# Head-by-head value products, earlier branch numbers and directly loaded gather indices in a two-layer graph network kernel

## The chip, the core and the metric

One core of one Trainium2 chip runs the whole program in one launch. The metric is the device time of one execution in microseconds.

## What is computed

Two graph layers over 6250 nodes of 160 channels (64 scalars and 32 vectors of three) and 200000 edges sorted by destination. What matters of the reference (LN and the matrices between are left out):

```python
# layer 0: attention
msg = (s_n @ Ws_src)[src] + (s_n @ Ws_dst)[dst]
w1 = rbf @ W_rbf
m1_s, m1_v = _cg_tp(msg_s, msg_v, y0, y1, w1[...])
a = jnp.sum(leaky((m1_s @ W_alpha).reshape(e, H, AS_)) * alpha_dot, axis=-1)
ex = jnp.exp(a - segment_max(a, dst)[dst]); alpha = ex / segment_sum(ex, dst)[dst]
m2_s, m2_v = _cg_tp(val_s, val_v, y0, y1, w2...)
h = concatenate([m2_s @ Ws_vlin, m2_v @ Wv_vlin])      # 4 heads of 40 columns
agg = segment_sum(alpha * h, dst)
# layer 1: mean over the edges of each destination
w = silu(edge_scalars @ Wfc1) @ Wfc2
e0, e1 = f0[src], f1[src]
n0..n3 = segment_mean(w * e * sh, dst)
```

## The kernel before, in words

**Groups.** Edges are taken in groups of 512 (four tiles of 128, edge on partition). Layer 0 has 391 groups, layer 1 has 392, two to a pair. Since the edges are sorted by destination, the sums of a group fall into a window of 128 nodes' worth of blocks, and a group whose nodes span more takes extra windows, in a loop behind a branch (`more_of` L663, `more_count` L660).

**Layer 0** runs under `schedule(step)` (L486): each of the five engines has its own program of the same steps, a step handles group g in several depths, and semaphores alone tie the engines together. In a step:

- SP (loads, one queue): `load_dst` L679 (destinations spread to all partitions, dst_bc), `load_y` L682, and `load_edge` for group g+4 (L674 to L676: rbf on 8 blocks of partitions, y twice), which waits until POOL has made the product edge of group g+2.
- POOL (gathers): `add_message` (L730, msg = got_src + got_dst of group g+2), `take_idx` (L714, copies the indices of group g+4 from the resident table idx_all into a small buffer and waits for its own copy), four indirect gathers (L720: two tiles, from src_tab and dst_tab), `scale_edge` (L737, edge = rbf * y), four more gathers. Eight gathers and two tensor operations to a group.
- PE: edge weights (`weigh` L767), transposes of msg (L773), `add_piece` L778, logits and weights turned (L791, L796), `sum_products` L802 (all 4 value parts times the softmax weights, summed into the window, 128 rows of which 32 belong to each head), and `project` L809, which multiplies the copied sums (held) by the value matrices. Its output has the four heads side by side, and of these the product of a head's rows with the other heads' columns is not used.
- DVE: `take_window` L990 picks from it, in four operations of 32 partitions, each head's own columns times two masks (side); `add_sums` L998 adds them to the running sums. It also makes blocks (L1030), product (L1053 and around), gated (L1134), near (L1095) and far (L1069, from dst_bc).
- ACT: copies out of PSUM, exponentials.

**Layer 1** runs under `by_fours(step)`. SP loads rbf, y_edge and 2 KB of indices to a group (L1463); POOL gathers four tiles (L1497); PE makes weights (L1516, L1527) and window sums (L1538); DVE makes to_node L1616, pre (L1625, L1629), along and val (L1641, L1647). After each second group DVE merges a pair's window into total (`merge`, `add_window` L1653, two operations): it reads the block number from a table in SBUF into a register (L1658), adds, then reads two window numbers (`more_of_pair` L1339, L1340) and branches; PE reads the same two and branches.

Of the kernel before, what the change touches and what calls it, by code (L numbers as in the profile page):

```python
# [15 lines left out]
I32 = mybir.dt.int32  # L16
ALU = mybir.AluOpType
# [494 lines left out]
def layer0(nc, ctx, A, K):  # L512
# [4 lines left out]
        "edge0", "edge1", "edge_y0", "edge_y1", "dst0", "dst1", "got0", "got1", "indexed", "summed", "scaled",  # L517
# [6 lines left out]
    with ExitStack() as sx:  # L524
# [120 lines left out]
        win = psum[3][:, 512:512 + HEADS * SB].rearrange("p (h c) -> p h c", h=HEADS)  # L645
# [22 lines left out]
        with nc.Block() as block:  # L668
            @block.sync
            def _(sp):  # L670
# [12 lines left out]

                def step(g, slot, use, now, mid, late):
                    if not now:
                        return
                    if not mid:
                        for first in range(2):
                            load_edge(first, first)
                        load_y(0, 0)  # L690
                        for first in range(2):
                            wait_apart(sp, s["scaled"], first + 1, s["tick_s"])
                            load_edge(first + 2, first)
                    if late:
                        wait_apart(sp, s["top"], g, s["tick_s"])
# [12 lines left out]
            def _(pool):  # L708
# [30 lines left out]
                def step(g, slot, use, now, mid, late):  # L739
# [12 lines left out]
                for first in range(2):  # L752
                    take_idx(first, first)
                    gather(first, range(TILES))
                for first in range(2):
                    add_message(first, first, 0, True)
                    scale_edge(first, first, 0, True)
                    take_idx(first + 2, first)
# [5 lines left out]
            def _(pe):  # L764
# [41 lines left out]
                def project():  # L806
                    for b in range(4):
                        cols = slice(0, SB) if b == 0 else slice(AS, HV)
                        last = nc.tensor.matmul(win[:, :, cols], held[:, P * b:P * b + P], w_val[:, b, :, cols],  # L809
                                                start=b == 0, stop=b == 3)  # L810
                    return last

                def step(g, slot, use, now, mid, late):
# [20 lines left out]
                    if late:  # L834
                        pe.wait_ge(s["sum_copied"], g - 1)
# [14 lines left out]
                        more_of(pe, g - 2, more_count(pe, g - 2), more)  # L850
# [116 lines left out]
            def _(dve):  # L967
# [869 lines left out]
```

## Time and profile before

| | us |
|---|---|
| median of 3 runs | 8944.23 (8936.49 to 8950.29) |
| the profiled execution | 8938.21 |
| its span | 8936.4 |
| PE busy in the span | 7983.1 (89%) |
| DVE busy | 7351.8 (82%) |
| POOL busy | 5977.1 (67%) |
| ACT busy | 3272.5 (37%) |

The span is one profiled execution; the rows below are of it. PE is matmul, PEld its weight loads (they overlap with PE), POOL the gathers and two tensor operations, SP the loads. A busy share is a mean over stages with different limits. Layer 0 runs from about 364 to 6255 us, layer 1 from about 6590 to 8870 us.

### The profile page before, as it was taken

Reading aid. Unit: us, or ns where it says so; the run is one execution under the profiler, and the core shown is the slowest. Engines: PE = TensorE matmul, PEld = TensorE weight load, DVE = VectorE, ACT = ScalarE, POOL = GpSimd, SP = SyncE. Lnnn points to the kernel's source line nnn. Section 1 sums busy time; section 2 is a strip of 40 time slices with the busy share of each in tenths; the row PEclk is TensorE's granted clock in tenths of the full one; section 3 lists DMA queues with packets and bytes.
Section 4 is the critical chain, followed back from the end, with each engine's and each line's share of the span. In section 5 each row is a group of like instructions: output and inputs, shape, how many; then the busy total and the mean of one; then the engine's idle time right before and its main releaser. Section 6 shows DMA issues by size and latency. Waiting matters only on the chain. (4 is left out here: it accounts for less than half of the span.)

```text
span 8936.4 us, 202775 instructions
## 1 busy us (share of the span) xinstructions
PE 7983.1 (89%) x50701; PEld 6094.9 (68%) x50702; DVE 7351.8 (82%) x18803; ACT 3272.5 (37%) x8375; POOL 5977.1 (67%) x5890
## 2 busy tenths in 40 slices
PE   2699999999999999999999999787968888888888
PEld 1488888888888888888888888666634444444445
DVE  4699999999999999999999999675368888887886
ACT  1244444444444444444444444332222222222223
POOL 0577777777777777777777777551046666666664
PEclk9799999999999999999999999898568888888888
DMA  3344444444444444444444433220012222222222
GB/s 54 78 99 99 98 98 99 98 99 98 99 98 99 98 98 99 99 98 99 98 99 98 99 98 98 66 70 23 11 43 65 64 65 65 64 65 64 65 64 58
DMA packets 616620, 725.49 MB, mean 81 GB/s; under 512 B 284132, under 2 KB 390884, under 8 KB 616573
## 3 DMA queue, kind: packets, MB, share of 16 engines
q0 software_dynamic: 225408, 385.00, 19.6%
q1 hardware_dynamic: 391165, 339.92, 15.0%
q8 instruction: 22, 0.36, 0.0%
q14 instruction: 25, 0.20, 0.0%
HBM read 708.40 MB, written 16.06 MB: 81 GB/s over the span
## 5 line engine op out<-in xcount | busy, mean ns | idle before, releaser
L720 POOL DMA_INDIRECT got_src<-src_tab,idx x1564 | 1773.3, 1134 | 659.3 <-POOL idx L714 358.4
L778 PE MATMUL bank_pair<-w_msg,blocks 128*128 128x160 f32 (+2 forms) x15640 | 2067.2, 288 | 61.3 <-DVE blocks L1030 61.3
L778 PEld LDWEIGHTS bank_pair<-w_msg,blocks 128*128 128x128 f32 x15640 | 1975.2, 192 | 100.3 <-DVE blocks L1030 95.5
L1497 POOL DMA_INDIRECT gotf<-f_tab,idx x1568 | 1536.2, 980 | 758.0 <-issue 466.2
L720 POOL DMA_INDIRECT got_dst<-dst_tab,idx x1564 | 1499.0, 958 | 529.3 <-issue 505.5
L802 PEld LDWEIGHTS bank_pair<-weights_t,product 128*128 128x128 f32 x12896 | 1496.5, 195 | 309.3 <-issue 294.9
L802 PE MATMUL bank_pair<-weights_t,product 128*128 128x128 f32 x12896 | 1573.3, 281 | 8.9 <-ACT weights_t L929 8.2
L1538 PE MATMUL bank_pair<-val,to_node 128*128 128x385 f32 x3136 | 1328.5, 573 | 2.7 <-DVE val L1647 2.7
L1589 ACT ACTIVATE val<-pre,y_edge 128x160 f32<-128x160 f32 x1568 | 542.7, 417 | 1618.6 <-DVE pre L1629 1614.7
L1538 PEld LDWEIGHTS bank_pair<-val,to_node 128*128 128x128 f32 x3136 | 658.1, 221 | 593.1 <-issue 348.7
L767 PE MATMUL bank_pair<-edge,w_edge 64*128 64x512 f32 x3128 | 884.8, 642 | 5.0 <-DVE blocks L1030 5.0
L936 ACT ACTIVATE rl<-bank_pair 128x256 f32<-128x256 f32 x391 | 150.2, 384 | 1801.9 <-PE bank_pair L778 1801.9
L1527 PE MATMUL bank_pair<-w_fc,hid 64*128 64x192 f32 x3136 | 399.1, 376 | 315.7 <-DVE val L1647 306.4
L897 ACT ACTIVATE product<-gated,y_edge 128x96 f32<-128x96 f32 x1564 | 458.1, 363 | 573.4 <-DVE gated L1134 573.2
L1527 PEld LDWEIGHTS bank_pair<-w_fc,hid 64*128 64x128 f32 x3136 | 272.7, 202 | 565.8 <-DVE val L1647 424.3
L737 POOL TENSOR_TENSOR edge<-rbf,y 128x512 f32<-128x512 f32 x391 | 500.8, 1281 | 234.6 <-PE bank_pair L778 227.5
L809 PEld LDWEIGHTS bank_pair<-w_val,held 128*128 128x128 f32 x3224 | 412.2, 190 | 307.2 <-ACT held L902 307.2
L730 POOL TENSOR_TENSOR msg<-got_src,got_dst 128x640 f32<-128x640 f32 x391 | 607.4, 1554 | 16.0 <-PE bank_pair L767 8.9
L990 DVE TENSOR_TENSOR win_scaled<-bank_pair,side 32x82 f32<-32x82 f32 x1612 | 384.8, 239 | 188.2 <-PE bank_pair L809 129.6
L1030 DVE TENSOR_TENSOR blocks<-bank_pair,turned_low 128x512 f32<-128x512 f32 x782 | 500.8, 680 | 32.5 <-PE bank_pair L767 28.1
L1030 DVE TENSOR_TENSOR blocks<-bank_pair,turned_high 128x512 f32<-128x512 f32 x782 | 502.1, 683 | 24.7 <-PE bank_pair L767 19.7
L1616 DVE TENSOR_TENSOR to_node<-iota_row,slot 128x512 f32<-128x512 f32 x392 | 270.6, 690 | 274.1 <-PE bank_pair L1538 141.7
(265 smaller groups left out, 12830.9 us busy)
## 6 DMA issues: line engine op xcount, KB each, us to landing
rbf<-in_rbf SPq DMA_DIRECT2D x391, 256.0 KB
dst_bc<-in_dst_rows SPq DMA_DIRECT2D x391, 256.0 KB
y<-in_y SPq DMA_DIRECT2D x391, 128.0 KB
y<-in_y SPq DMA_DIRECT2D x391, 96.0 KB
gotf<-f_tab,idx POOLq DMA_INDIRECT x1568
got_src<-src_tab,idx POOLq DMA_INDIRECT x1564
got_dst<-dst_tab,idx POOLq DMA_INDIRECT x1564
rbf<-in_rbf SPq DMA_DIRECT2D x392, 32.0 KB
```

The costliest lines, as they stand in the source:

```text
L720: pool.indirect_dma_start(out=buf[slot][:, t, :], out_offset=None, in_=table[:, :], in_offset=bass.IndirectOffsetOnAxis(ap=idx[slot][:, c: ...
L730: pool.tensor_tensor(msg[slot][:], got_src[slot][:], got_dst[slot][:], ALU.add).then_inc(s["summed"], 1)
L737: pool.tensor_tensor(edge[slot][:], rbf8[slot][:], y8[slot][:], ALU.mult).then_inc(s["scaled"], 1)
L767: nc.tensor.matmul(ebank[half], w_edge[r, pair, :], weigh.operand[r, :], start=True, stop=True).then_inc(s["weighed"], 1)
L778: return nc.tensor.matmul(to, blocks[rows, k, P * t:P * t + P], w_msg[rows, c0:c1], start=start, stop=stop)
L802: last = nc.tensor.matmul(sum_bank[:, P * b:P * b + P], product[slot][:, t, b, :], weights_t[:, t, :], start=t == 0, stop=t == TILES - 1)
L897: last = nc.scalar.activation(product[slot][:, t, 1:4, 64:96], gated[:, t, CS:D].rearrange("p (x c) -> p x c", x=3), ACT.Copy, scale=y_edg ...
L1030: dve.tensor_tensor(blocks[:, k, :], ebank[k % 2], (turned_low, turned_high)[k // 2][:], ALU.mult).then_inc(s["block_done"], 1)
L1497: pool.indirect_dma_start(out=got[k][:, t, :], out_offset=None, in_=f_tab[:, :], in_offset=bass.IndirectOffsetOnAxis(ap=idx[k][:, t:t + 1] ...
L1527: last = nc.tensor.matmul(weights[k % 2][:, t, 0:192], hid[k % 2][r, P * (t % 2):P * (t % 2) + P], K["w_fc2"][r, :], start=True, stop=True)
L1538: last = nc.tensor.matmul(win[k // 2], to_node[k % 2][:, t, :], val[k][:, t, :], start=k % 2 == 0 and t == 0, stop=k % 2 == 1 and t == TIL ...
L1589: last = nc.scalar.activation(val[k][:, t, 0:D], pre[:, t, 0:D], ACT.Copy, scale=y_edge[k][:, t, 0:1])
```

## The change

Three parts.

**Value products by head.** `project` (now L818) makes, for each of its 4 parts, four matmuls: head h's 32 columns of held as weights, that head's 41 or 24 value columns as the moving side, out to PSUM rows 32h to 32h+31. `take_window` is one operation on 128 partitions.

**Gather indices of layer 0.** POOL's copy and its wait go. SP loads 128 x 8 indices (4 KB) from DRAM into the same two small buffers, four groups ahead, at the head of its step; POOL waits for that load, then for msg (summed).

**Branch numbers.** In layer 0 PE reads its count ahead of the wait for sum_copied. In layer 1 block number and count are packed in one table (marks1); each engine reads one number early, and the second only inside the branch.

```diff
-        win = psum[3][:, 512:512 + HEADS * SB].rearrange("p (h c) -> p h c", h=HEADS)
+        win = psum[3][:, 512:512 + SB]
...
+                def load_idx(g, slot):
+                    sp.dma_start(idx[slot][:], group_of(A["idx"], g)).then_inc(s[f"idx{slot}"], 16)
+
                 def step(g, slot, use, now, mid, late):
...
                         for first in range(2):
+                            load_idx(first, first)
+                        for first in range(2):
                             load_edge(first, first)
                         load_y(0, 0)
                         for first in range(2):
+                            wait_apart(sp, s[f"got{first}"], 128, s["tick_s"])
+                            load_idx(first + 2, first)
+                        for first in range(2):
                             wait_apart(sp, s["scaled"], first + 1, s["tick_s"])
                             load_edge(first + 2, first)
+                    if not (isinstance(g, int) and g + 4 >= NG):
+                        wait_apart(sp, s[f"got{slot}"], use * 128 + 256, s["tick_s"])
+                        load_idx(g + 4, slot)
                     if late:
                         wait_apart(sp, s["top"], g, s["tick_s"])
                     load_dst(g, slot)
...
-                def take_idx(g, slot):
-                    pool.tensor_copy(idx[slot][:], idx_all[:, bass.ds(g, 1), :].rearrange("p a c -> p (a c)")).then_inc(s["indexed"], 1)
-                    wait(s["indexed"], g + 1)
...
                     add_message(g + 2, slot, use + 1, False)
                     if further:
-                        take_idx(g + 4, slot)
+                        wait(s[f"idx{slot}"], use * 16 + 48)
                         wait(s["summed"], g + 3)
                         gather(slot, (0, 1))
...
-                        last = nc.tensor.matmul(win[:, :, cols], held[:, P * b:P * b + P], w_val[:, b, :, cols],
-                                                start=b == 0, stop=b == 3)
+                        for h in range(HEADS):
+                            r = slice(BLK * h, BLK * h + BLK)
+                            last = nc.tensor.matmul(win[r, cols], held[:, P * b + BLK * h:P * b + BLK * h + BLK], w_val[:, b, h, cols],
+                                                    start=b == 0, stop=b == 3)
...
                     if late:
+                        count = more_count(pe, g - 2)
                         pe.wait_ge(s["sum_copied"], g - 1)
                         project().then_inc(s["projected"], 1)
...
-                        more_of(pe, g - 2, more_count(pe, g - 2), more)
+                        more_of(pe, g - 2, count, more)
...
-                    for h in range(HEADS):
-                        r = slice(BLK * h, BLK * h + BLK)
-                        last = dve.tensor_tensor(win_scaled[r, :, :], win[r, h, :].unsqueeze(1).broadcast_to([BLK, 2, SB]),
...
-                    return last
+                    return dve.tensor_tensor(win_scaled[:], win.unsqueeze(1).broadcast_to([P, 2, SB]),
+                                             side[:, at_group(g), :].rearrange("p a c -> p (a c)").unsqueeze(2).broadcast_to([P, 2, SB]),
+                                             ALU.mult)
...
-def more_of_pair(eng, more_from, q):
-
-    return (eng.value_load(more_from[0:1, at_pair(q)], min_val=0, max_val=MAX_W),
-            eng.value_load(more_from[0:1, at_pair(q + 1)], min_val=0, max_val=MAX_W))
+def more_of_pair(eng, more_from, q, count, body):
+
+    with eng.If(count > 0):
+        first = eng.value_load(more_from[0:1, at_pair(q)], min_val=0, max_val=MAX_W)
+        body(first, first + count)
...
+        def mark_of(eng, q):
+            return eng.value_load(marks[0:1, at_pair(q)], min_val=0, max_val=2 ** 12 - 1)
...
+                    if merging:
+                        count = mark_of(pe, i * 2 + k // 2 - 1) >> 6
                     if not (fixed and g + 1 >= NG_PAD):
                         make_weights(i + (k + 1) // 4, (k + 1) % 4)
...
+                    mark = mark_of(dve, i * 2 + k // 2 - 1) if merging else None
                     dve.wait_ge(s["along"], g * 3 + 2)
...
-                    row = dve.value_load(block_i[0:1, at_pair(q)], min_val=0, max_val=NT - 1)
+                    row, count = nc.s_assert_within(mark & 63, 0, NT - 1), mark >> 6
```

How it moves the work at three places. First SP in the steady loop of layer 0, one step, before:

```order
L679 ISA [waits l0_top]
L679 DMA dst_bc<-in_dst_rows 128x512
L682 ISA [waits l0_product,l0_scaled_y]
L682 DMA y_edge<-in_y_edge 128x20
L674 ISA [waits l0_scaled]
L674 DMA rbf<-in_rbf 128x1x512
L675 ISA
L675 DMA y<-in_y 64x1x512
L676 ISA
L676 DMA y<-in_y 48x1x512
```

and now:

```order
L674 DMA rbf<-in_rbf 128x1x512
L675 ISA
L675 DMA y<-in_y 64x1x512
L676 ISA
L676 DMA y<-in_y 48x1x512
L685 ISA [waits l0_got1]
L685 DMA idx<-in_idx 128x8
L679 ISA [waits l0_top]
L679 DMA dst_bc<-in_dst_rows 128x512
```

The new load idx stands straight behind the three edge loads of the step before and ahead of the wait for dst_bc.

Second POOL in the same loop, around the first gather of a step, before:

```order
L730 TENSOR_TENSOR msg<-got_src,got_dst 128x640 [waits l0_weighed]
L714 ISA
L714 COPY idx<-idx_all 128x8
L70 REGISTER_ALU
L70 REGISTER_ALU [waits l0_indexed]
L720 DMA got_src<-src_tab,idx 128x160 [waits l0_summed]
```

and now:

```order
L737 TENSOR_TENSOR msg<-got_src,got_dst 128x640 [waits l0_weighed]
L70 ISA
L70 REGISTER_ALU [waits l0_idx0]
L727 DMA got_src<-src_tab,idx 128x160 [waits l0_summed]
L727 DMA got_dst<-dst_tab,idx 128x160
```

The copy is gone, and the wait for it is one for SP's load.

Third DVE in the steady loop of layer 1, at the merge of a pair (total is the table of sums), before:

```order
L1645 TENSOR_TENSOR along<-along 128x4x32 [waits l1_along]
L1646 REGISTER_ALU
L1647 TENSOR_TENSOR val<-along,bank_pair 128x4x32 [waits l1_along]
L1658 ISA
L1658 TENSOR_LOAD block_i
L1658 ISA x2
L1659 ISA
L1653 ISA [waits l1_merged,l1_window_sum]
L1653 SCALAR_TENSOR_TENSOR total<-bank_pair,here,total 128x385
L1653 ISA
L1653 SCALAR_TENSOR_TENSOR total<-bank_pair,after,total 128x385
L1339 REGISTER_ALU
```

and now:

```order
L1659 TENSOR_TENSOR val<-pre,y_edge 128x4x192 [waits l1_first_half]
L1465 ISA
L1465 TENSOR_LOAD marks
L1465 ISA x2
L1663 REGISTER_ALU
L1664 TENSOR_TENSOR along<-along 128x4x32 [waits l1_along]
L1665 REGISTER_ALU
L1666 TENSOR_TENSOR val<-along,bank_pair 128x4x32 [waits l1_along]
L1678 REGISTER_ALU x2
L1678 ISA
L1679 ISA
L1673 ISA [waits l1_merged,l1_window_sum]
```

The one load stands two products earlier, and the two loads of more_from that followed L1653 (each L1339 or L1340 ISA, TENSOR_LOAD, ISA x2) are now one, behind the branch.

## Rows read from the trace of the kernel before

**Rows 1.** Busy us (x instructions) of each engine by stretch; PEclk, DMA share, GB/s last
```profile
core 0: us, PE busy (x) PEld busy (x) DVE busy (x) ACT busy (x) POOL busy (x), PEclk, DMA share, GB/s
...
1000.00:5500.00 4500.00, 4363.99 (x32448) 3710.36 (x32448) 4094.89 (x11233) 1942.63 (x4680) 3539.18 (x3432) 1.00 0.41 98
...
5590.00:6255.00 665.00, 512.47 (x3482) 441.94 (x3482) 422.68 (x1227) 195.57 (x465) 272.21 (x265) 0.87 0.21 53
```

**Rows 2.** Groups of POOL by line and shape, 1000 to 5500 us: busy, mean ns | idle
```profile
L720 POOL DMA_INDIRECT got_src<-src_tab,idx x1248 | 1428.4, 1145 | 526.0 <-POOL idx L714 286.2 <-issue 239.8
L720 POOL DMA_INDIRECT got_dst<-dst_tab,idx x1248 | 1187.8, 952 | 423.4 <-issue 402.7 <-PE bank_pair L767 20.7
L730 POOL TENSOR_TENSOR msg<-got_src,got_dst 128x640 f32<-128x640 f32 x312 | 484.1, 1551 | 5.4
L737 POOL TENSOR_TENSOR edge<-rbf,y 128x512 f32<-128x512 f32 x312 | 399.6, 1281 | 6.0
L714 POOL COPY idx<-idx_all 128x8 int32 x312 | 60.1, 193 | 0.0
```

**Rows 3.** Timeline of POOL from 3003.7 us: start, duration, [idle before <-releaser]
```profile
3003.72 1.55 POOL L730 TENSOR_TENSOR msg<-got_src,got_dst 128x640 f32<-128x640 f32 x1
3005.20 0.19 POOL L714 COPY idx<-idx_all 128x8 int32 x1
3006.34 0.98 POOL L720 DMA_INDIRECT got_src<-src_tab,idx  x1 [0.95 <-POOL idx L714]
...
3011.21 1.28 POOL L737 TENSOR_TENSOR edge<-rbf,y 128x512 f32<-128x512 f32 x1
...
3020.12 0.98 POOL L720 DMA_INDIRECT got_src<-src_tab,idx  x1 [0.89 <-POOL idx L714]
```

**Rows 4.** Timeline of SP's queue, same stretch
```profile
3012.77 0.65 SPq L674 DMA_DIRECT2D rbf<-in_rbf  x1
...
3014.54 0.77 SPq L676 DMA_DIRECT2D y<-in_y  x1
```

**Rows 5.** Groups of DVE and POOL by line, layer 1, 7000 to 8443 us
```profile
L1616 DVE TENSOR_TENSOR to_node<-iota_row,slot 128x512 f32<-128x512 f32 x249 | 171.9, 690 | 175.5 <-PE bank_pair L1538 91.3 <-issue 81.7
...
L1653 DVE SCALAR_TENSOR_TENSOR total<-bank_pair,here,total 128x385 f32 x125 | 77.4, 619 | 96.8 <-issue 55.1 <-PE bank_pair L1538 41.7
...
L1497 POOL DMA_INDIRECT gotf<-f_tab,idx x997 | 976.0, 979 | 467.7 <-issue 298.0 <-DVE val L1647 169.7
```

**Rows 6.** DMA issues of the page: KB each
```profile
rbf<-in_rbf SPq DMA_DIRECT2D x391, 256.0 KB
...
y<-in_y SPq DMA_DIRECT2D x391, 128.0 KB
y<-in_y SPq DMA_DIRECT2D x391, 96.0 KB
```

**Rows 7.** Layer 1's index load (L1463), issue to landing
```profile
DMA to landing us min/median/max: 1.5/1.6/1.9
```

**Rows 8.** Timeline of SP's queue at the start of layer 0
```profile
337.98 0.61 SPq L674 DMA_DIRECT2D rbf<-in_rbf  x1
...
340.03 0.43 SPq L679 DMA_DIRECT2D dst_bc<-in_dst_rows  x1
...
357.85 0.65 SPq L674 DMA_DIRECT2D rbf<-in_rbf  x1
```

**Rows 9.** Timeline of DVE at the start of layer 0, line L1069
```profile
346.37 0.49 DVE L1069 TENSOR_SCALAR far<-dst_bc,ring 128x512 f32<-128x512 int32 x1 [2.76 <-DMA dst_bc<-in_dst_rows]
...
367.23 0.48 DVE L1069 TENSOR_SCALAR far<-dst_bc,ring 128x512 f32<-128x512 int32 x1 [6.07 <-DMA dst_bc<-in_dst_rows]
```

**Rows 10.** Timeline of PE's weight loads at project()
```profile
3001.62 1.02 PEld L809 LDWEIGHTS bank_pair<-w_val,held 128*128 128x128 f32 x8 [0.76 <-ACT held L902]
```

**Rows 11.** Group of DVE, 1000 to 5500 us
```profile
L990 DVE TENSOR_TENSOR win_scaled<-bank_pair,side 32x82 f32<-32x82 f32 x1248 | 297.9, 239 | 47.5 <-issue 25.5
```

**Rows 12.** DVE's queue at line L1339, 7000 to 8443 us: duration ns min/median/max
```profile
L1339 DVEq TENSOR_LOAD <-more_from x125: 298/303/316, 7001.5 to 8438.5; - x125
L1339 DVEq FUSED_REGOPS  x125: 190/190/190, 7001.9 to 8438.8; - x125
```

More of the change, by code:

```diff
@@ L752, in _ @@
                 for first in range(2):
-                    take_idx(first, first)
+                    wait(s[f"idx{first}"], 16)
                     gather(first, range(TILES))
@@ L757, in _ @@
                     scale_edge(first, first, 0, True)
-                    take_idx(first + 2, first)
+                    wait(s[f"idx{first}"], 32)
                     wait(s["summed"], first + 1)
@@ L1385, in _ @@
                 def _(dve):
-                    chain = Chain(dve, s["step"], 25)
+                    chain = Chain(dve, s["step"], 27)
                     chain.begin(0)
@@ L1540, in sum_window, with more_of, body @@
                     last.then_inc(s["window_sum"], 1)
-                def more_of(i, k):
+                def more_of(i, k, count):
                     q, half = i * 2 + k // 2, k // 2
-                    first, end = more_of_pair(pe, more_from, q)
-                    with pe.If(first < end):
+                    def body(first, end):
                         with pe.Fori(first, end) as w:
@@ L1552, in more_of @@
                             wait_apart(pe, s["more_added"], w + 1, s["tick_p"])
+                    more_of_pair(pe, more_from, q, count, body)
                 def step(i, k):
@@ L1561, in step @@
                         make_raw(0, 2)
+                    merging = k % 2 == 1 and not (fixed and g < 2)
+                    if merging:
+                        count = mark_of(pe, i * 2 + k // 2 - 1) >> 6
                     if not (fixed and g + 1 >= NG_PAD):
@@ L1567, in step @@
                         sum_window(i + (k + 3) // 4 - 1, (k + 3) % 4)
-                    if k % 2 == 1 and not (fixed and g < 2):
-                        more_of(i + (k + 2) // 4 - 1, (k + 2) % 4)
+                    if merging:
+                        more_of(i + (k + 2) // 4 - 1, (k + 2) % 4, count)
                     if fixed and g == NG_PAD - 1:
                         sum_window(i, k)
-                        more_of(i, k)
+                        more_of(i, k, mark_of(pe, i * 2 + k // 2) >> 6)
                 by_fours(step)(pe)
@@ L1662, in merge, with body @@
                     add_window(half, q, row).then_inc(s["merged"], 1)
-                    first, end = more_of_pair(dve, more_from, q)
-                    with dve.If(first < end):
+                    def body(first, end):
                         wait_apart(dve, s["merged"], q + 1, s["tick_v"])
@@ L1667, in merge @@
                             more(half, q, row, first, w, y0_done)
+                    more_of_pair(dve, more_from, q, count, body)
                 def more(half, q, row, first, w, y0_done):
@@ L1697, in step @@
                         make_hidden(0, 1)
-                    products(i, k)
-                    if k % 2 == 1 and not (fixed and g < 2):
-                        merge(i + (k + 2) // 4 - 1, (k + 2) % 4, g + 1)
+                    merging = k % 2 == 1 and not (fixed and g < 2)
+                    mark = products(i, k, merging)
+                    if merging:
+                        merge(i + (k + 2) // 4 - 1, (k + 2) % 4, g + 1, mark)
                     if fixed and g == NG_PAD - 1:
-                        merge(i, k, g + 1)
+                        merge(i, k, g + 1, mark_of(dve, i * 2 + k // 2))
                 by_fours(step)(dve)
```

18 lines of the change are left out of this document (10 added, 8 removed).

## The prediction

> **What bounds the kernel now.** First the table of busy time by stage [rows 1]: 1000 to 5500 us is layer 0 at its steady pace, 5590 to 6255 us is its end, where single groups take extra windows; layer 1 follows from 6590 us. In the first stage POOL ran 3432 operations, eleven to a group, so 312 groups in 4500 us: **14.42 us a group**. PE is busy for 4364.0 of the 4500 and DVE for 4094.9. POOL shows 3539.2, but its five kinds of row [rows 2] with the idle before them (1428.4 + 526.0, 1187.8 + 423.4, 484.1 + 5.4, 399.6 + 6.0, 60.1) sum to 4526 us, or the whole stage: what stands before a gather is issue, and the wait for its own index copy. So in layer 0 POOL is full too, and PE, DVE and POOL end within a few per cent of each other. That makes it a place where a saving on one engine buys little and a new wait on any buys its full length.
>
> POOL's loop is read from its timeline [rows 3]. A sum msg ends at 3005.27, the copy idx at 3005.39, the first gather starts 0.95 later, at 3006.34. Two pairs of gathers follow, then the product edge, which ends at 3012.49, 6.15 after that first gather. Four more gathers, the next msg, and the next first gather starts at 3020.12. On SP [rows 4] the three loads of edge inputs start at 3012.77, 0.28 after the product edge, and the last is issued by 3015.31. SP's next work is dst_bc.
>
> In layer 1, 997 gathers, four to a group, passed in 1443 us: 249 groups, so **11.59 us a pair** of groups. DVE's idle stands before L1653 (96.8 us, 0.77 a pair) and before the next L1616 (175.5 us, 1.41 a pair) [rows 5], the two places where it reads branch numbers.
>
> **The change, part by part. Indices of the gathers.** The copy L714 (0.19) and the wait on it (0.95) leave POOL; in their place SP issues a 4 KB load at the head of its step, and POOL waits for it after msg. It is issued at 3015.4 on the clock of the rows, behind 480 KB of edge inputs on the same queue [rows 6]. POOL needs it at 3019.17, 0.95 before the gather at 3020.12, which is 6.40 after the start of the rbf issue (3012.77). Is it there? No row of layer 0 has such a load, so it is bounded.
> - From below, layer 1's own index load, 2 KB with no large load ahead, lands 1.5 to 1.9 us after issue [rows 7]: 3017.3, in time, and POOL loses 1.14 less one semaphore wait.
> - From above, the start of layer 0, where dst_bc is issued straight behind such loads [rows 8] and DVE stands waiting for it [rows 9]. The rbf issue starts at 337.98 and L1069 at 346.37, 8.39 later; the second time 357.85 and 367.23, 9.38 later. The first dst_bc issue began at 340.03, so this load with edge inputs ahead took 6.3 us from its own issue, against 1.6 alone.
>
> I take 8.3, by the nearest rows: same queue, same loads ahead; a little under 8.39 because dst_bc has 128 x 512 values, 256 KB, of its own to move and the new load has 4 KB. The rule of the Trainium skill that speaks for this is in "DMA: Bandwidth & Descriptors", section "Queues, rings and completion order": on each DMA engine descriptors are consumed in ring order, and one issuing engine has one ring there, so a small load cannot overtake. The two starts of L1069 agree.
>
> The loop then runs first gather to end of edge 6.15, to the rbf issue 0.28, to the landing 8.3, to the gather 0.95: **15.68 us**, 1.26 over 14.42. The full pace holds from 364 to 5590 us, 362 groups, of which the first four have loads with nothing ahead: 358 x 1.26 = **+451 us**. It would feed on itself: the load is issued behind the edge inputs, these wait for the product edge, and that for the gathers. At the end of the layer (665 us for the last 29 groups) PE is held by the extra windows and POOL catches up; there the extra windows hide the wait, and PE and DVE gain a little: **-30**.
>
> **project().** Its four matmuls become sixteen of 32 weight columns; in passes, 8 become 32. Before, eight weight loads take 1.02 us [rows 10]. From below: if the four heads' quarters of the array run beside one another, under half of it; from above: with no overlap between load and multiply, 1.7. The nearest row is the present one, and with weight loads a quarter as wide I take 1.0, no change. Its cover is POOL's wait, 1.26 a group; without that, up to 0.7 a group would show. The count's load moves ahead of the wait for sum_copied, where nothing waits for it: nothing.
>
> **take_window.** Four operations of 239 ns with 47.5 us of idle in 312 groups [rows 11], 1.11 us a group, become one. The nearest row is its own: the one has the 82 columns of each, on 128 partitions instead of 32, so about 0.24 to 0.3. DVE gains 0.8 us a group, all of it hidden behind POOL: nothing.
>
> **Layer 1.** A load of a branch number takes DVE's queue 0.30 us and its unpacking 0.19 [rows 12]. Before L1653 one such pair is on the path, 0.49 of the 0.77; it moves beside L1641 and goes. After the second L1653 two pairs and a branch stand, beginning beside its 0.61; now one branch. Of the 1.41 before L1616 part is PE's (91.3 of 175.5), since PE's sums are ready late; and PE gets its own number early too. I take half of it, 0.5 to 0.7. Together about 1.0 a pair. Late next is POOL: eight gathers of 0.98 with 0.30 of issue each, 10.2 [rows 5], against the new 10.6. 190 of 196 pairs: **-190 us**; bounds, -80 (the first load alone) and -260 (POOL's pace). Metadata: two short steps, +1.
>
> **The sum:** 8938 (the profiled execution, 6 under the median of the runs) + 451 - 30 - 190 = 9169; against the median, **9175 us**.
>
> **The rivals.**
> - **The index load comes in time, so faster.** Mechanism: the 4 KB rides past the edge loads and lands by 3019.17, 6.40 after the rbf issue, instead of 8.3. Place: POOL's first gather. POOL then loses 0.3 to 1 us a group, DVE 0.8, and PE's 4364 us, 13.99 a group, is next, less what it was stretched. 0.5 x 390 = -195, with -190: 8553, about 8550. For it: layer 1's row, 1.6. Against: both starts of L1069. [...] Chance 0.12.
> - **Late, but less.** If the edge inputs, not dst_bc's own 256 KB, are done 6.4 to 7.4 us after the rbf issue, the loop is 13.8 to 14.8: layer 0 moves between -195 and +130, and the whole ends at 8550 to 8850, likeliest 8800. The decision against the forecast's sign is at 7.65, where the loop (15.03) costs what layer 1 gives. Chance 0.08.
> - **project() becomes the bound.** Index load in time, passes with no overlap: PE 13.99 + 0.7 = 14.7 a group, layer 0 +0.25 x 390 = +100, with -190: 8850. Chance 0.02.
>
> **How the numbers follow.** Forecast 0.78. Its own range: landings of 7.6 to 9.0 after the rbf issue, loops of 15.0 to 16.4, layer 0 +200 to +700, less 30 and 80 to 260: 8890 to 9430 (the full 9.38 would be 9550). The range given reaches down to 8850, part of the second rival, and leaves out the first. A run of this kernel can be told from no change at about 0.2%, 18 us. Faster 0.21 (the rivals less a little), same 0.02, slower 0.77.
>
> **What would show it.** Right: POOL's idle before the first gather of each group released by the DMA of idx and about 1.9 us longer than msg to copy before; PE's busy time in layer 0 down from 14.0 us of 14.4 to 14 of 15.7 with waits for POOL's edge; a period near 15.7; layer 1 near 10.6 a pair with the idle before L1653 halved. Wrong: an index load that lands within 4 us of its issue, or a POOL wait put down to edge inputs. If the period is over 16.5, the landing, not the sum, was mis-sized.

## The result, and the profile after

The changed kernel takes **9369.85 us** (median of 4 runs, 9368.09 to 9385.23) beside 8940.36 us before on the same chip (8928.25 to 8950.29): a ratio of 1.0485, 95% interval 1.0467 to 1.0503. It is slower, as forecast, and inside the range, but by 429 us where the sum said 231.

The stage row of the changed kernel for layer 0 at its steady pace (columns as in [rows 1]):

```profile
1000.00:5500.00 4500.00, 3934.86 (x36019) 3295.43 (x36007) 3768.43 (x9284) 1722.20 (x4217) 3363.43 (x2816) 0.97 0.36 89
```

and POOL's groups by line and shape in the same stretch, to be laid beside [rows 2]:

```profile
L727 POOL DMA_INDIRECT got_dst<-dst_tab,idx x1126 | 1428.3, 1268 | 377.5 <-issue 372.0 <-PE bank_pair L774 5.5
L727 POOL DMA_INDIRECT got_src<-src_tab,idx x1127 | 1139.3, 1011 | 751.6 <-DMA idx<-in_idx 519.6 <-issue 215.2 <-POOL msg L737 15.6
L737 POOL TENSOR_TENSOR msg<-got_src,got_dst 128x640 f32<-128x640 f32 x281 | 436.4, 1553 | 4.7
L744 POOL TENSOR_TENSOR edge<-rbf,y 128x512 f32<-128x512 f32 x282 | 361.0, 1280 | 4.8
```

In 4500 us 281.6 groups passed instead of 312: **15.98 us a group**, against 14.42. There is a releaser that [rows 2] does not have: 519.6 us of POOL's idle, 1.85 a group, end with the DMA of idx. The loop itself, in POOL's timeline and then in that of SP's queue:

```profile
3007.87 1.07 POOL L727 DMA_INDIRECT got_src<-src_tab,idx  x1 [1.96 <-DMA idx<-in_idx]
...
3012.70 1.28 POOL L744 TENSOR_TENSOR edge<-rbf,y 128x512 f32<-128x512 f32 x1
...
3015.44 2.64 POOL L727 DMA_INDIRECT got_dst<-dst_tab,idx  x1 [0.30 <-issue]
...
3024.00 1.09 POOL L727 DMA_INDIRECT got_src<-src_tab,idx  x1 [1.85 <-DMA idx<-in_idx]
```

```profile
3014.21 0.68 SPq L674 DMA_DIRECT2D rbf<-in_rbf  x1
...
3017.39 0.35 SPq L685 DMA_DIRECT2D idx<-in_idx  x1
3018.12 0.33 SPq L679 DMA_DIRECT2D dst_bc<-in_dst_rows  x1
```

First gather 3007.87, product edge done at 3013.98 (6.11), rbf issued at 3014.21 (0.23), next first gather at 3024.00 (9.79): 16.13 in this group. Over the 250 groups of 1000 to 5000 us the three pieces average 6.28, 0.23 and 9.47, together 15.98, and in 233 of them the first gather was released by the DMA of idx. By its semaphore the load is down 8.58 us after the rbf issue and 5.66 after its own (medians); the gather starts 0.94 later. Nothing else of the three engines stands in that chain. That the queue holds the loads back shows in the list of DMA issues of 1000 to 5000 us (KB each, median us from issue to landing):

```profile
dst_bc<-in_dst_rows SPq DMA_DIRECT2D x250, 256.0 KB, 5.4
idx<-in_idx SPq DMA_DIRECT2D x250, 4.0 KB
y_edge<-in_y_edge SPq DMA_DIRECT2D x250, 10.0 KB, 5.4
```

The load y_edge has 10 KB and takes 5.4 us; it, too, is now issued behind the edge inputs, and behind dst_bc besides. SP no longer stands waiting for DVE before dst_bc: it gets there later than DVE is done. The Trainium skill, "DMA: Bandwidth & Descriptors", section "Queues, rings and completion order", has descriptors consumed in ring order on each engine; the trace agrees in these 5.4 us, against 1.7 for y_edge with nothing ahead (e1 below).

Taken from the first gather of a layer to its last, layer 0 ran 5804 us before and 6333 us after (+529), layer 1 2257 and 2175 (-82). The remaining -17 us of the two spans' difference, 430, lie in the stages between and at the end.

Layer 1 of the changed kernel, 7400 to 8843 us, groups of POOL and DVE, for [rows 5]:

```profile
L1511 POOL DMA_INDIRECT gotf<-f_tab,idx x1040 | 1127.5, 1084 | 317.0 <-issue 317.0
```

```profile
L1643 DVE TENSOR_TENSOR pre<-bank_pair,gotf 128x512 f32<-128x512 f32 x260 | 179.7, 691 | 158.0 <-DMA gotf<-f_tab,idx 157.3
L1634 DVE TENSOR_TENSOR to_node<-iota_row,slot 128x512 f32<-128x512 f32 x260 | 178.6, 687 | 22.9 <-PE bank_pair L1552 22.9
...
L1673 DVE SCALAR_TENSOR_TENSOR total<-bank_pair,here,total 128x385 f32 x130 | 80.5, 619 | 35.3 <-issue 35.3
```

DVE's idle at the two merge places fell from 0.77 and 1.41 us a pair to 0.27 and 0.18, 1.7 together, which is more than forecast; yet the pair takes 11.10, only 0.49 less. The rest came back as a new wait of 158.0 us (1.22 a pair) for the gathered rows, and POOL's 1127.5 + 317.0 fill the whole 1443 us: POOL is the pace. PE's granted clock in layer 1 rose as well, from 0.87 to 0.94 of full; whether that is a part of the shorter idle or follows from it, no run separates.

### The profile page after: what moved, and what is told of

The parts are those of the page before. It is cut to its first block and busy times, and to the rows that moved or that the text cites. A ratio compares the mean times of both kernels' runs of the same rounds, so it can differ in the third digit from the quotient of the medians.

```text
span 9366.3 us, 219066 instructions
## 1 busy us (share of the span) xinstructions
PE 7792.0 (83%) x60373; PEld 5931.0 (63%) x60374; DVE 7437.6 (79%) x17597; ACT 3234.1 (35%) x8375; POOL 6354.4 (68%) x5499
## 5 line engine op out<-in xcount | busy, mean ns | idle before, releaser
L785 PE MATMUL bank_pair<-w_msg,blocks 128*128 128x160 f32 (+2 forms) x15640 | 2247.0, 303 | 521.6 <-DVE blocks L1037 517.9
L785 PEld LDWEIGHTS bank_pair<-w_msg,blocks 128*128 128x128 f32 x15640 | 2140.8, 204 | 613.2 <-DVE blocks L1037 612.8
L727 POOL DMA_INDIRECT got_src<-src_tab,idx x1564 | 1585.2, 1014 | 1070.6 <-DMA idx<-in_idx 749.3
L727 POOL DMA_INDIRECT got_dst<-dst_tab,idx x1564 | 1953.2, 1249 | 523.3 <-issue 515.7
L1511 POOL DMA_INDIRECT gotf<-f_tab,idx x1568 | 1698.6, 1083 | 514.5 <-issue 477.7
L1552 PE MATMUL bank_pair<-val,to_node 128*128 128x385 f32 x3136 | 1237.6, 541 | 4.8 <-DVE val L1666 4.8
L1552 PEld LDWEIGHTS bank_pair<-val,to_node 128*128 128x128 f32 x3136 | 616.8, 207 | 532.4 <-issue 263.2
L1076 DVE TENSOR_SCALAR far<-dst_bc,ring 128x512 f32<-128x512 int32 x391 | 197.6, 505 | 446.4 <-DMA dst_bc<-in_dst_rows 445.3
L1141 DVE TENSOR_TENSOR gated<-vec,gates 128x384 f32<-128x384 f32 x391 | 471.1, 1205 | 13.5
L1060 DVE TENSOR_TENSOR product<-gated,y_edge 128x1024 f32<-128x1024 f32 x391 | 476.5, 1219 | 0.0
```

What stands on the lines that cost most here:

```text
L727: pool.indirect_dma_start(out=buf[slot][:, t, :], out_offset=None, in_=table[:, :], in_offset=bass.IndirectOffsetOnAxis(ap=idx[slot][:, c: ...
L785: return nc.tensor.matmul(to, blocks[rows, k, P * t:P * t + P], w_msg[rows, c0:c1], start=start, stop=stop)
L1060: dve.tensor_tensor(to[:, :, :, 0:CS], gated[:, :, 0:CS].unsqueeze(2).broadcast_to(by_s), y[:, :, 0:4].unsqueeze(3).broadcast_to(by_s), AL ...
L1511: pool.indirect_dma_start(out=got[k][:, t, :], out_offset=None, in_=f_tab[:, :], in_offset=bass.IndirectOffsetOnAxis(ap=idx[k][:, t:t + 1] ...
L1552: last = nc.tensor.matmul(win[k // 2], to_node[k % 2][:, t, :], val[k][:, t, :], start=k % 2 == 0 and t == 0, stop=k % 2 == 1 and t == TIL ...
```

## The experiments

e1 to e4 ran on a chip where the kernel before took 8938 us. e5 to e8 ran on a second, where it took 10319 us, and e9 to e12 on a third, where it took 10302 us. Ratios are to the kernel before on the same chip; the changed kernel itself was not run on the two slower ones. Periods are counts of gathers in 4000 us of layer 0, or 1400 us of layer 1.

### e1: POOL's copy back, the rest as changed

```diff
-                        wait(s[f"idx{slot}"], use * 16 + 48)
+                        take_idx(g + 4, slot)
...
-                    if not (isinstance(g, int) and g + 4 >= NG):
-                        wait_apart(sp, s[f"got{slot}"], use * 128 + 256, s["tick_s"])
-                        load_idx(g + 4, slot)
```

> The change with its index part undone: POOL copies the indices from the resident table again, everything else as changed. Theory (the late index load is the whole slowdown): layer 0 loses the 1.57 us a group that it gained (15.99 in the changed kernel against 14.42 before) and DVE's saving shows, so 13.9 us a group; about 9370 - 360 x 2.1 = 8610 us. Rival (the 32 short passes of project, or the changed window operation, hold layer 0): period stays over 14.4, 8800 us or more. Layer 1 as in the changed kernel in both, 11.1 us a pair.

Measured: **8686.21 us**, ratio 0.9723 (0.9706 to 0.9740); 14.0 us a group, 11.12 a pair: the theory's, not the rival's. The total is 76 us over what I gave; layer 0 lost 712 us to the changed kernel (6333 to 5621) where I had 756, and the profiled execution of the run was itself a quick one, 8658. So the index part costs 9370 - 8686 = 684 us, and the other two parts gain 252: in layer 0 their gain stood behind the new wait. The stage row, and the 10 KB load y_edge, which in this kernel is issued 3.7 us behind dst_bc and well ahead of the edge inputs:

```profile
1000.00:5000.00 4000.00, 3850.47 (x36533) 3211.32 (x36533) 3684.78 (x9420) 1767.04 (x4285) 3121.14 (x3141) 1.00 0.43 101
```

```profile
y_edge<-in_y_edge SPq DMA_DIRECT2D x286, 10.0 KB, 1.7
```

1.7 us here, 5.4 in the changed kernel: same load, same bytes, other things ahead.

### e2: the index load ahead of the edge loads

```diff
+                    if not (isinstance(g, int) and g + 5 >= NG):
+                        wait_apart(sp, s[f"got{1 - slot}"], (use + slot) * 128 + 256, s["tick_s"])
+                        load_idx(g + 5, 1 - slot)
                     if not (isinstance(g, int) and g + 4 >= NG):
                         wait_apart(sp, s["scaled"], g + 3, s["tick_s"])
                         load_edge(g + 4, slot)
```

> The changed kernel with SP's index load moved by one place, from straight behind the three edge loads to straight ahead of them (for the group after, since its buffer is free by then). Theory (it is late because it stands behind 480 KB on its own queue): POOL's wait for the DMA of idx goes, layer 0 runs at 13.9 us a group or a little under, since POOL has lost its copy too; 8550 to 8620 us. Rival (DVE's new wait for dst_bc, 445 us in the changed kernel, is a second pace-maker because SP now does other loads first): idx wait gone but DVE's wait for dst_bc stays, 15 us or more a group, over 9000 us.

Measured: **8729.55 us** (8704.96 to 8806.72), ratio 0.9786 (0.9729 to 0.9844), 14.18 us a group. One place earlier in the same queue takes 640 us off the changed kernel. POOL's wait for the DMA of idx is gone, and so is DVE's for dst_bc, so that wait was a follower. By the packet records the last of the 128 pieces of 32 bytes is through 1.3 us (median) after the issue, and 4.7 us in the changed kernel. Missed: it is not as fast as I gave (8550 to 8620); it stands a little over e1, though POOL has one operation less. POOL's rows show where it went, of this kernel and then of e1:

```profile
L730 POOL DMA_INDIRECT got_src<-src_tab,idx x1128 | 1264.2, 1121 | 439.4 <-POOL msg L740 222.8 <-issue 210.9 <-PE bank_pair L777 5.8
L730 POOL DMA_INDIRECT got_dst<-dst_tab,idx x1129 | 1105.2, 979 | 384.0 <-issue 360.5 <-PE bank_pair L777 23.5
```

```profile
L720 POOL DMA_INDIRECT got_src<-src_tab,idx x1143 | 1188.9, 1040 | 481.2 <-POOL idx L714 261.5 <-issue 213.6 <-PE bank_pair L767 6.1
L720 POOL DMA_INDIRECT got_dst<-dst_tab,idx x1142 | 1087.8, 953 | 386.9 <-issue 357.9 <-PE bank_pair L767 29.0
...
L714 POOL COPY idx<-idx_all 128x8 int32 x285 | 55.0, 193 | 0.0
```

Four gathers each of 1.121 and 0.979 us against 1.040 and 0.953 are 0.43 us a group more, more than the 0.35 that the copy and the longer wait after it had cost (0.19, and 0.95 instead of 0.79).

### e3: the index load between rbf and the y loads

```diff
                     sp.dma_start(rbf8[slot][:], rows.unsqueeze(0).broadcast_to([8, NB, GE])).then_inc(s[f"edge{slot}"], 16)
+                    if between:
+                        between()
```

> The index load stands behind the first edge load (rbf, 256 KB) and ahead of the two y loads. Queue theory: its landing follows rbf's only, so it comes between those of e2 and the changed kernel, about 4 to 5 us after the start of the rbf issue; POOL needs it at 6.4, so no wait is left and layer 0 runs as in e2, 13.9 us; the y loads and so the product edge are not late either. Rival (4 KB in 128 pieces of 32 bytes takes over 5 us wherever it stands): landing 6.2 us or more after the rbf issue, idle of POOL before its first gather 0.9 to 1.2 with part of it put down to the DMA of idx, 14.0 to 14.5 us a group.

Measured: 8728.28 us, ratio 0.9772 (0.9754 to 0.9790), 14.22 us a group, as e2 and not the 13.9 that I gave. The last index packet ends 3.3 us after its issue and 4.2 after rbf's (medians): between e2 and the changed kernel, in the queue theory's 4 to 5 and below the rival's 6.2. The size of the delay follows what stands ahead.

### e4: only two edge loads ahead

```diff
-                    sp.dma_start(y8[slot][80:128, :], y[1:4, :].unsqueeze(1).broadcast_to([3, NB, GE])).then_inc(s[f"edge{slot}"], 16)
+                    if isinstance(g, int) and g < 2:
+                        sp.dma_start(y8[slot][80:128, :], y[1:4, :].unsqueeze(1).broadcast_to([3, NB, GE])).then_inc(s[f"edge{slot}"], 16)
```

> The changed kernel, index load in its place behind the edge loads, but the third of these (96 KB, the lower part of y) is made only for the first two groups; all later groups use those values, so this leaves a part of the input out. Queue theory: a third less queued ahead on the engines that carry all three, so the index load lands 2 us or more earlier (0.8 of it because it is issued earlier) and layer 0 runs at 14.0 us a group, about 8650 us. Rival (its own slowness, 5.4 us from issue to landing): only the 0.8 us of the earlier issue is won, 15.2 us a group, about 9080 us.

Measured: **9051.27 us**, ratio 1.0130 (1.0113 to 1.0147), 15.16 us a group: the rival's number, not mine. The packets do not bear the rival out: the last one ends 6.2 us after the rbf issue against 7.7 in the changed kernel, 1.5 earlier, of which the earlier issue is about 1.1 (it is 4.3 after its own issue against 4.7). That is less than the 2 us that I gave to one load of three. POOL's wait for the DMA of idx fell to 103.2 us in 264 groups, 0.4 each, so the landing is not what holds most groups. POOL's rows, for e2's above:

```profile
L728 POOL DMA_INDIRECT got_dst<-dst_tab,idx x1055 | 1237.7, 1173 | 356.3 <-issue 355.7 <-PE bank_pair L775 0.6
L728 POOL DMA_INDIRECT got_src<-src_tab,idx x1056 | 1190.6, 1128 | 455.0 <-issue 196.3 <-POOL msg L738 148.9 <-DMA idx<-in_idx 103.2
```

Of the 0.98 us a group over e2, 0.80 are longer gathers (4 x 0.194 and 4 x 0.007) and 0.17 the idle before got_src. Why the gathers are longer stands in POOL's timeline and DVE's:

```profile
3007.54 2.58 POOL L728 DMA_INDIRECT got_src<-src_tab,idx  x1 [0.30 <-issue]
```

```profile
3007.41 1.22 DVE L1061 TENSOR_TENSOR product<-gated,y_edge 128x1024 f32<-128x1024 f32 x1
3008.54 0.29 DVE L1064 TENSOR_TENSOR product<-product,along 128x128 f32<-128x128 f32 x1
3008.74 0.56 DVE L1065 TENSOR_TENSOR product<-product,across 128x384 f32<-128x384 f32 x1
```

A gather that starts 0.13 us after the start of DVE's three products takes 2.58 us instead of 0.95 and is out only after they are; the same in the changed kernel (3015.44, 2.64 us, the products from 3015.36). In the kernel before, one gather began 0.28 ahead of the products (3007.62 against 3007.90) and took 0.95, the next 0.98 into them and took 1.06. In 4000 us of layer 0 this repeats: the 237 gathers of e4 that begin within 0.3 us behind the start of the products average 2.32 us, the 228 of the changed kernel 2.37, and the 258 of the kernel before that begin 0.1 to 0.9 ahead of them 0.95. Gathers of over 2 us number 0 in e1, 22 in e2, 75 in the kernel before, 140 in the changed kernel and 149 in e4. The Trainium skill, "SBUF — State Buffer", section "Who interferes with whom", says that a DVE operation with two SBUF inputs contends with a GpSimd operation that reads SBUF, the shared port pair being an exclusive lock; these rows agree that the gather waits. Where the gather began first (3007.62, the kernel before), neither took longer: the product has its 1.22 us in both. In the changed kernel these long gathers lie in a part of the group that the wait for idx hides. That the stretch is what makes e4's 15.16 follows from the rows; no run took it away.

### e5 and e9: the index part alone

The kernel before with this part of the diff; e9 is the same kernel once more.

```diff
-                        take_idx(g + 4, slot)
+                        wait(s[f"idx{slot}"], use * 16 + 48)
...
+                        wait_apart(sp, s[f"got{slot}"], use * 128 + 256, s["tick_s"])
+                        load_idx(g + 4, slot)
```

> The kernel before with only the index part of the change (SP loads them behind the edge loads; four-matmul project, four window operations and the old branch numbers stay). Theory (one loop sets layer 0: product edge, edge loads, landing of the indices behind them, four gathers, product edge; PE and DVE stand beside it): period 15.9 to 16.1 us as in the changed kernel, though PE and DVE have more to do; layer 1 11.59; total 9370 + 95 = 9465 us. Rival (PE's or DVE's part is in the loop, and the project part gave back 0.4 a group in the changed kernel): 16.4 us a group, about 9620 us.

> The same kernel as in the earlier run of the index part alone, since on that run's chip every kernel took 15% longer, the one before too. Theory (one loop: product edge, edge loads, landing behind them, four gathers): 16.0 us a group as in the changed kernel, whatever PE and DVE have to do; about 9465 us where the kernel before takes 8938. Rival (the project part gave back part of the index part's cost): 16.4 us, 9620 us.

Measured: 10267.58 us (e5; one of its six runs took 10054.14, so it has no interval, and e9 is the one to go by) beside 10319.42 before, and 10255.52 us (e9), ratio 0.9956 (0.9940 to 0.9973). The period is 16.6 and 16.7 us, neither theory's number, but the loop is the theory's. In 1000 to 5000 us of e9, 239 of 240 first gathers are released by the DMA of idx, and the three pieces of the loop average 6.97, 0.23 and 9.48 us, together 16.68 (e5: 7.13, 0.23, 9.27). Against the changed kernel on the first chip (6.28, 0.23, 9.47) only the first piece is longer: its four gathers take 4.6 us together there and 3.95 here. POOL's row of e9:

```profile
L727 POOL DMA_INDIRECT got_src<-src_tab,idx x960 | 1098.2, 1144 | 917.0 <-DMA idx<-in_idx 732.0 <-issue 179.8 <-PE bank_pair L774 3.1
```

That is 3.05 us a group of waiting for the load, and yet the part costs next to nothing: with the old POOL copy the second chip needs 16.61 a group too (e7), where POOL's sum and product edge wait for PE instead, 284.5 and 127.4 us in 241 groups. Whether the parts' costs add up on the first chip was not tried there, beyond e1.

### e6 and e10: project and the window operation alone

```diff
-                        last = nc.tensor.matmul(win[:, :, cols], held[:, P * b:P * b + P], w_val[:, b, :, cols],
+                        for h in range(HEADS):
+                            r = slice(BLK * h, BLK * h + BLK)
+                            last = nc.tensor.matmul(win[r, cols], held[:, P * b + BLK * h:P * b + BLK * h + BLK], w_val[:, b, h, cols],
```

> The kernel before with only the project part (sixteen matmuls by head, one window operation). The run with the index part undone had 14.0 us a group in layer 0 against 14.42 and 8686 us; if all of that gain of layer 0 is this part's: 14.0 a group, 8938 - 155 = 8785 us, layer 1 unchanged at 11.59 a pair. Rival (the gain was the count's load on PE moved ahead of the wait): 14.42 here, 8938 us.

> The project part alone once more, for the same reason. Theory (the gain of layer 0 in the run with the copy back is this part's): 14.0 us a group, 11.59 a pair, about 8785 us where the kernel before takes 8938. Rival: 14.42, no change.

Measured: 10482.91 us, ratio 1.0158 (1.0127 to 1.0189), and 10481.91, ratio 1.0179 (1.0145 to 1.0212): **slower** by 1.6 and 1.8%, 17.2 and 17.3 us a group, and neither theory had that. PE's timeline of e10 and then of e1:

```profile
3016.17 0.46 PE L811 MATMUL bank_pair<-w_val,held 128*32 128x41 f32 x32 [1.56 <-ACT held L904]
3017.62 0.66 PE L791 MATMUL bank_pair<-ident,logits_wide 128*128 128x128 f32 x2 [0.99 <-issue]
```

```profile
3009.80 0.46 PE L811 MATMUL bank_pair<-w_val,held 128*32 128x41 f32 x32
3010.54 0.63 PE L791 MATMUL bank_pair<-ident,logits_wide 128*128 128x128 f32 x4 [0.28 <-issue]
```

The 32 passes take 0.46 us, where the eight took 1.07 to the next operation before ([rows 10] has their weight loads). As the rows read, the load of the count, its unpacking and the branch ran beside the long form and are bare behind the short one: 0.99 us of issue. 0.46 + 0.99 against 1.07 is 0.38 us a group more on PE, near the 163 and 180 us in 391 groups, 0.42 and 0.46, that the part costs. In e1 the count is read ahead of project and 0.28 remains. The test is e11 (below) beside e10, on one chip: in layer 0 they differ in nothing but the early count, and e11 takes 16.45 us a group, 0.88 less. So the early count in layer 0, which I had put at nothing, is what lets project's gain through.

PE's clock has a part in it that I had not looked at. Over 1000 to 5000 us the granted clock is 0.90 of full in e10, 0.93 in e11, 0.98 in e7 and 1.00 in e1. In e10 it is at its lower level (0.50, 1.2 GHz) from 3000.3 to 3003.7 us, after an idle of 1.01 us behind project, and the 34 passes that follow take 5.72 us where e1's take 4.45 at the upper level (2.4 GHz):

```profile
3000.95 5.72 PE L778 MATMUL bank_pair<-w_msg,blocks 128*128 128x160 f32 x34
```

```profile
3011.25 4.45 PE L778 MATMUL bank_pair<-w_msg,blocks 128*128 128x160 f32 x34
```

How much of the 0.88 us goes through the clock, no run separates.

### e7: the branch numbers alone

```diff
+                        count = more_count(pe, g - 2)
                         pe.wait_ge(s["sum_copied"], g - 1)
...
-                    row = dve.value_load(block_i[0:1, at_pair(q)], min_val=0, max_val=NT - 1)
+                    row, count = nc.s_assert_within(mark & 63, 0, NT - 1), mark >> 6
```

> The kernel before with only the branch numbers moved, in both layers. Theory: nothing in layer 0 (14.42 a group), 11.1 us a pair in layer 1, where POOL's gathers become the pace: 8938 - 95 = 8843 us. Rival (layer 0 gains from PE's early count): 14.0 a group and 8690 us.

Measured: 10214.96 us, ratio 0.9899 (0.9875 to 0.9924); 16.61 us a group, 13.73 a pair. Faster by 1.0%, as the theory's 1.1%, but not at its pace: on the two slower chips layer 1 gave 14.0 to 14.3 a pair with the old numbers (e5, e6, e9, e10) and 13.7 to 13.8 with the new ones (e7, e8, e12). The kernel before has no trace there, so what layer 0 gained alone stays open.

### e8 and e12: the index load on ScalarE's queue

```diff
+                    if now and not (isinstance(g, int) and g + 4 >= NG):
+                        wait_apart(act, s[f"got{slot}"], use * 128 + 256, s["tick_a"])
+                        act.dma_start(idx[slot][:], group_of(A["idx"], g + 4)).then_inc(s[f"idx{slot}"], 16)
```

> The changed kernel, but from group 4 on the index load is issued by ScalarE on its own DMA queue, at the point of its step where it waits for PE's scalars. Queue theory: nothing of its own queue is ahead of it, its packets are done within 2 us of the issue although the edge loads are under way on SP's queue, POOL never waits for it, 14.1 to 14.2 us a group as with the load ahead of the edge loads, about 8730 us. Rival (not the queue but the DMA engines themselves are full while the edge inputs pass): packets end 4 us or more after the issue.

> The index load on ScalarE's own DMA queue as in the earlier run, but issued ahead of ScalarE's wait for PE's window sums; there it came behind that wait, only 0.4 us ahead of POOL's msg, and POOL waited 2.3 us although the packets were done 2.5 us after the issue. Queue theory: no wait of POOL for the DMA of idx, 14.1 to 14.2 us a group and about 8730 us where the kernel before takes 8938. Rival (a DMA load issued by ScalarE costs its own step more than it saves): over 14.5 us a group.

Measured: e8 10352.72 us, ratio 1.0033 (1.0017 to 1.0050), 17.1 us a group; e12 **10071.32 us**, ratio 0.9795 (0.9767 to 0.9823), 16.4 us. The kernels differ only in that e12 issues ahead of ScalarE's wait for the window sums; they ran on the second and the third chip. The diff is e8's; e12 has the same lines further up. In e8 the load came too late by its place in ScalarE's program: the issue, and the gather that waited for it,

```profile
3000.99 0.34 ACTq L943 DMA_DIRECT2D idx<-in_idx  x1
```

```profile
3005.31 0.97 POOL L724 DMA_INDIRECT got_src<-src_tab,idx  x1 [2.34 <-DMA idx<-in_idx]
```

In e12 POOL waits for its own msg alone:

```profile
POOL got_src L724 <- POOL msg L734: 96.4, 122, 0.8
```

The last index packet ended 1.3 us after the issue in e8 (median; 3.1 or more in a quarter of the groups) and 3.5 in e12, 4.7 behind the edge loads on SP's queue. These compare moments as much as queues: e8's load is issued 6.9 us after rbf (median), when the edge inputs have passed, e12's 0.8 after it. On SP's own queue and at the same moment, 0.9 behind rbf, e3's last packet ended 3.3 us after the issue. So in the landing no gain of the own queue shows; what e12 has over the changed kernel is the earlier issue. At e12's moment the 3.5 us lie nearer to the 4 us of e8's rival (DMA engines full while the edge inputs pass) than to the theory's 2. e12's ratio to before is about that of e2 (0.9786), on another chip.

### e11: three gathers a group in layer 1

```diff
-                    for t in range(TILES):
+                    for t in range(TILES if isinstance(i, int) and i == 0 else TILES - 1):
```

> The changed kernel with POOL's copy of the indices back, and in layer 1 only three of the four gathers of a group (the fourth tile keeps the rows of the first four groups, so a part of the input is left out). In layer 1 of the changed kernel POOL is full: 8 gathers of 1.08 with 0.30 between them are 11.1 us a pair. Theory (POOL's gathers, stretched from 0.98 by the closer packed DVE, are what ate half of the gain I forecast): with 6 of them, 8.3 us, DVE's work becomes the pace, 10.2 to 10.5 us a pair, 8686 - 150 = 8535 us. Rival (PE and DVE wait for one another at 11.1): no change, 8686 us.

Measured: **9325.12 us**, ratio 0.9063 (0.9036 to 0.9090). A pair takes 9.79 us, where e12, with four gathers and the same layer 1 otherwise, takes 13.66 on the same chip: nearly 4 us for two gathers less, far more than either theory. The stage rows of 7600 to 8600 us, e11 and then e12:

```profile
7600.00:8600.00 1000.00, 873.92 (x4082) 462.50 (x4080) 947.19 (x2042) 345.03 (x1020) 608.78 (x613) 1.00 0.27 59
```

```profile
7600.00:8600.00 1000.00, 733.71 (x2901) 381.66 (x2900) 674.10 (x1450) 245.18 (x725) 587.65 (x580) 0.83 0.24 54
```

With three gathers DVE is busy for 947 of 1000 us, so DVE's work is the pace, as the theory says; and PE's granted clock is 1.00 instead of 0.83. The gathers' number matters to layer 1, then, but with four of them no engine is full on this chip, so the run does not show that POOL is the pace there; on the first chip POOL's rows, which fill the stage, say so. How much of the 4 us goes through PE's clock is open, since gathers, DMA traffic and clock changed together. The theory's "closer packed DVE" is not enough as a reason for longer gathers: in e11 DVE is the busiest of all, and a gather takes 0.99 us.

## Why the prediction was right, and where its sizes were off

**The mechanism held.** POOL full in layer 0; the index load behind the edge inputs; a loop of product edge, edge loads, landing, four gathers. Every link is in the timeline, and moving the load by one place (e2) or giving the copy back (e1) removes the loss.

**The loop was 0.30 us too short.** Its terms were 6.15 from the first gather to the end of the product edge, 0.28 to the rbf issue, and 8.3 to the landing plus 0.95 to the gather; measured are 6.28, 0.23 and 9.47, in all 15.98 for 15.68. The 0.22 in the last term is SP's: it issues the index load 2.94 us after rbf in the mean (2.70 in one group, 3.19 in the next, as in the timeline above), not 2.63, while from its own issue the load is down after 5.66, as 8.3 less 2.63 has it. The 0.13 in the first term are longer gathers. 0.30 x 358 = 107 us of the 108 by which layer 0 (+529 against +421) was under-estimated. The upper bound, 9.38 plus 0.95, was not reached.

**Layer 1 was over-estimated by more than half**: -82 of the forecast -190. The step that failed is POOL's pace. I named POOL as next and priced its gathers at the 0.98 us of [rows 5], 10.2 a pair, under DVE's 10.6; they take 1.084, and 8 x (1.084 + 0.305) = 11.1. The reason lies in where they fall. In 7400 to 8800 us of the changed kernel 472 of 1007 gathers begin beside the DVE operations L1651 and L1659, which have two SBUF inputs, and average 1.22 us; before, 182 of 966 begin beside the same two operations and average 1.09; nearly all others take 0.95 to 0.99 in both. The lower bound of 80 held, barely.

The two errors add: 107 + 108 is the distance from 231 to 429, but for 17 us at the stages between and the end. The range fits its own terms loosely: +200 to +700, less 30 and 80 to 260, add up to 8848 and 9528, not 8890 and 9430; 9370 is inside both.

**project() was wrong in size and right in effect.** I took 1.0 us, no change; it is 0.46, the lower bound's case. The passes overlap: in e1 they start 5 to 32 ns apart and last 183 to 224 ns each, and the same 904 columns go through in less than half the time. The window operation is one of 233 ns in the changed kernel, as forecast. Both were hidden behind POOL's wait, as said; e1 shows what they and the early count are worth in the open, 183 us in layer 0 (5804 to 5621).

**The count in layer 0 was not nothing.** Alone it may be, but the short project() lays the old load bare: 0.99 us at e10, and 0.88 a group between e10 and e11.

**The rivals.** The load in time (0.12) is out: it was down 8.6 us after the rbf issue, where 6.4 was the limit. Late but less (0.08), up to 7.4, is out by the same number. project() as bound (0.02) is out on the first chip, where it takes 0.46 and e1 runs at 14.0 a group.

## What to carry to other kernels

A small load that someone waits for belongs ahead of the large ones in its queue, or early enough on any queue; its price is what stands ahead of it, not its bytes, and the row to look for is a small neighbour's time to landing. When an engine's idle is removed, price the next engine's operations by their times beside each kind of neighbour's operation and not by their old mean, since the mix will shift. A register load that costs nothing behind eight long passes costs its full length when these become short: an edit that shortens work should look at what ran beside it. Of the versions tried, the change without its index part (e1) is the fastest, 8686 us.

## What the runs showed that I had not expected

- A gather that starts just after the first of three DVE operations with two SBUF inputs waits for the whole run of them: 2.58 and 2.64 us instead of 0.95. One that starts 0.4 to 1.0 us into the run takes 1.5 on average in the kernel before. Which phase the two engines lock into is worth more than a POOL operation of 0.19 us: e2 has less work on POOL than e1 and is not faster.
- Two chips ran the kernel before some 15% slower than the first (10319 and 10302 against 8938 us), and the kernels tried on them took 16.4 to 17.3 us a group in layer 0 and 13.7 to 14.3 a pair. Two things differ in the traces. In layer 1, with four gathers a group, PE's granted clock is 0.81 to 0.83 there, and 0.87 before and 0.94 after the change on the first chip. In layer 0 PE's sums are late: in e10 they are recorded from 3009.71 for 3.84 us, at full clock (1.00 from 3004 to 3017), and ScalarE's copy of them starts at 3015.52, 2 us after their recorded end. From the start of the last sum to that copy it is 0.31 us in e1 and in the kernel before, and 2.2 to 2.3 in e7, e10, e11 and e12 (medians); in e5 and e9 it is 0.44. What makes them late is not settled. The verdict on a part depends on it: the index part costs 684 us on the first chip (by e1, beside the other two parts) and nothing on the third (alone, e9), and the project part alone costs 1.6 to 1.8% on the slower two.
- In layer 1 of the third chip, with two gathers less in a pair, PE's granted clock went from 0.83 to 1.00 and 4 us a pair went.
